# Self-attention of a decoder layer: denominators from the value product's weights, a new order on VectorE and ScalarE, and the residual addition on GpSimd

## The chip, the cores and the metric

The kernel runs on one core of one Trainium2 chip. The metric is the device time of one execution in microseconds. The kernel before takes 1735.19 us (median of 3 runs, 1734.19 to 1737.6). The engines are called PE (TensorE), DVE (VectorE), ACT (ScalarE), POOL (GpSimd) and SP (SyncE). Each has its own instruction stream, and semaphores join them.

## The reference, cut to what matters

Inputs are `x` (128 sequences of 64 tokens of 128 features, float32) and a context of the same shape. Three blocks follow each other, each with a layer norm ahead of it and its result added to `x`:

```python
x = x + attn(layernorm(x), Wq, Wk, Wv)         # self-attention: the stage that is changed
x = x + xattn(layernorm(x), ctx, ...)          # two LSTM cells with attention, 64 steps in sequence
x = x + ffn(layernorm(x), router_W, ...)       # top-1 of 8 experts

def attn(x, Wq, Wk, Wv):                       # 16 query heads of 8 features, one shared key and value head
    q = (x @ Wq.T).reshape(B, S, 16, 8).transpose(0, 2, 1, 3)
    k = x @ Wk.T;  v = x @ Wv.T
    p = softmax(einsum('bhqd,bkd->bhqk', q, k) / sqrt(8))
    return einsum('bhqk,bkd->bhqd', p, v).transpose(0, 2, 1, 3).reshape(B, S, 128)
```

## The kernel before, in words

The program has stages with a barrier between them: weights and context projections (to about 82 us), self-attention (to about 527 us), the second layer norm, the recurrence, and the experts. Only the self-attention stage is touched, lines 364 to 693.

All of `x` lies in SBUF as `X`. One pair of sequences fills 128 partitions (64 tokens each), so the stage works on 64 pairs. After a preparation (norm statistics, weights split into two float16 parts), each engine runs `step(i, u)` for i from -3 to 64; `run_steps` writes the first five and the last five steps out and puts the rest in a loop that holds two steps. In step i the engines work on several pairs at once:

- PE (L467): transposes the normalised rows of pair i+2 into `psK` (L473); scores of pair i+1, 32 small float16 products into `psSc` (L460); transposes `pv`, the value product of pair i-1, back into `psSc` (L487, four blocks); transposes the probabilities of pair i into `psT` (L492, eight blocks); projections of pair i+2 into `psQ` and `psK` and values of pair i+1 (all L453, by `split3`); and the value product of pair i (L520).
- The value product multiplies the transposed probabilities `prT` by two small stationary matrices of 32 columns: `VB` (for each of the two sequences and two heads, the 8 value features, zero on the other head's keys) and `ob` (ones in the same pattern, whose product is the softmax denominators). Both run over all 128 columns of `prT`, so of each result the half that combines a sequence's values with the other sequence's queries is thrown away. That makes 16 matmuls per pair for each matrix in instruction count (float32 products are issued as two), and `pv` has 512 columns: 256 of values and 256 of denominators.
- ACT (L537): `pv` copy of pair i-1 (L542), `xh`, the high part of the transposed input of pair i+2 (L546), two copies of `prT` (L551), `hq` (L557) and `hk` (L559), the high parts of the projections, and the exponential of pair i+1 (L563).
- DVE (L618): `xh` low part (L622), `xn` of pair i+3 (L628), `bn_stats` of the finished row of pair i-2 (L633), row maximum of the scores of pair i+1 (L642), reciprocal of the denominators (L648) and product into `yv` (L655) of pair i-1, each in two instructions of 64 partitions because the useful half of the columns differs by sequence, subtraction of the maximum (L664), `KS` (L670), `QS` (L672), `VB` (L678), and the addition of `yv` to `X` (L687).

Every engine takes its instructions in the order written. The waits that matter: `psK` of pair i+2 (L473) waits for `QS` and `VB` of DVE, since these read the same PSUM bank; ACT's `xh` waits for it, and DVE's `xh` for ACT's. The maximum (L642) waits for the scores and for the transposes of `pv` of pair i-1. `KS` waits for `hk`. The exponential waits for the subtraction, and the eight transposes (L492) of the next step wait for the exponential. GpSimd does nothing in this stage.

Of the kernel before, what the change touches and what calls it, by code (L numbers as in the profile page):

```python
# [14 lines left out]
P = 128  # L15
# [35 lines left out]
def decoder_kernel(nc, x, ctxT, wqT, wkT, wvT, wi0T, wh0T, bi0, bh0, wi1T, wh1T, bi1, bh1,  # L51
# [4 lines left out]
    with ExitStack() as persist:  # L56
# [307 lines left out]
        with ExitStack() as c2:  # L364
# [14 lines left out]
            ob = sb("ob", [P, 2, 2, DK])  # L379
# [10 lines left out]
            VB = sb("VB", [P, 2, 2, 2, DK])  # L390
# [3 lines left out]
            pv = sb("pv", [P, 512])  # L394
            rden = sb("rden", [P, NH])
            yv = sb("yv", [P, NH, DK])
# [32 lines left out]
            v_x1 = sem("v_x1")  # L429
# [6 lines left out]
            def run_steps(eng, step):  # L436
                for i in range(-3, 2):
                    step(i, i % 2)
                with eng.Fori(2, NPAIR - 5, 2) as i:
                    step(i, 0)  # L440
                    step(i + 1, 1)
                for i in range(NPAIR - 4, NPAIR + 1):
                    step(i, i % 2)

            with nc.Block() as block:
                @block.tensor
                def _(pe):
                    pe.wait_ge(v_c, 5)
# [18 lines left out]
                    def step(i, u):  # L467
# [11 lines left out]
                        if has(i - 1):  # L479
                            n = i - 1  # L480
                            pe.wait_ge(a_o, n + 1)
                            wait(pe, v_y, 2 * n)
                            if has(i) and not has(i + 1):
                                pe.wait_ge(v_sub, i + 1)
                            for k in range(4):
                                c0 = 256 + k % 2 * P
                                mm = nc.tensor.transpose(psSc[:, k // 2, c0:c0 + P], pv[:, k * P:(k + 1) * P], ident[:, :])  # L487
                            mm.then_inc(p_ot, 1)
# [38 lines left out]
                def _(act):  # L527
# [3 lines left out]
                    act.wait_ge(v_c, 5)  # L531
# [35 lines left out]
                def _(dve):  # L567
# [11 lines left out]
                    for b in range(2):  # L579
                        nc.vector.tensor_copy(ob[:, b, :, :], pm[:, :].unsqueeze(2).broadcast_to([P, 2, DK])).then_inc(v_c, 1)  # L580
                    dve.wait_ge(v_c, 5)
# [12 lines left out]
                    dve.wait_ge(v_c, 7)  # L594
# [23 lines left out]
                    def step(i, u):  # L618
                        if has(i + 2):
                            n = i + 2  # L620
                            dve.wait_ge(a_xh, n + 1)
                            nc.vector.scalar_tensor_tensor(xh[:, u, 1, :], psK[:, 0:P], S, xh[:, u, 0, :],  # L622
                                                           ALU.mult, ALU.subtract).then_inc(v_xl, 1)
                        if has(i + 3):
                            n = i + 3
                            wait(dve, p_xt, n - 1)
                            wait(dve, v_x1, i - 1)
                            nc.vector.tensor_scalar(xn[:, 1 - u, :], X[:, bass.ds(n * D, D)], mvf[:, bass.ds(n * 2, 1)],  # L628
                                                    rs[:, bass.ds(n, 1)], ALU.subtract, ALU.mult).then_inc(v_xn, 1)
                        if has(i - 2):  # L630
                            if not has(i + 3):
                                dve.wait_ge(v_x1, i - 1)
                            nc.vector.bn_stats(x1_stf[:, bass.ds((i - 2) * 6, 6)],  # L633
                                               X[:, bass.ds((i - 2) * D, D)]).then_inc(v_x1st, 1)
# [8 lines left out]
                        if has(i - 1):  # L643
                            n = i - 1
                            dve.wait_ge(p_ot, n + 1)
                            for b in range(2):
                                q = slice(64 * b, 64 * b + 64)
                                nc.vector.reciprocal(  # L648
                                    rden[q, :].rearrange("p (k h) -> p k h", h=2),
                                    psSc[q, 1, 256:512].rearrange("p (k b h d) -> p k b h d", b=2, h=2, d=DK)[:, :, b, :, 0]  # L650
                                ).then_inc(v_rd, 1)
                            dve.wait_ge(v_rd, 2 * n + 2)
                            for b in range(2):
                                q = slice(64 * b, 64 * b + 64)
                                nc.vector.tensor_tensor(  # L655
                                    yv[q, :, :].rearrange("p (k h) d -> p k h d", h=2),
                                    psSc[q, 0, 256:512].rearrange("p (k b h d) -> p k b h d", b=2, h=2, d=DK)[:, :, b, :, :],
                                    rden[q, :].rearrange("p (k h) -> p k h", h=2).unsqueeze(3).broadcast_to([64, 8, 2, DK]),
                                    ALU.mult).then_inc(v_y, 1)
# [7 lines left out]
                        if has(i + 2):  # L667
                            n = i + 2
                            dve.wait_ge(a_hq, 2 * n + 2)
                            nc.vector.scalar_tensor_tensor(KS[:, u, :], psK[:, P:2 * P], DOWN, hk[:, :],  # L670
                                                           ALU.mult, ALU.subtract)
                            nc.vector.scalar_tensor_tensor(QS[:, u, :], psQ[:, :], DOWN, hq[:, :],  # L672
                                                           ALU.mult, ALU.subtract).then_inc(v_qs, 1)
                        if has(i + 1):
# [4 lines left out]
                                VB[:, 1 - u, :, :, :],  # L679
# [10 lines left out]
                    dve.wait_ge(v_x1, NPAIR)  # L690
# [1033 lines left out]
```

## Time and profile before

| | |
|---|---|
| median of 3 runs | 1735.19 us |
| the profiled execution | 1734.93 us, span 1733.2 us |
| busy in the span: PE, DVE, ACT, POOL | 1453.0, 1191.0, 749.5, 401.6 us |
| mean granted TensorE clock, whole span | 0.929 |
| self-attention, 128 to 512 us: PE, DVE, ACT, POOL busy | 288.27, 319.47, 232.25, 0.00 of 384 us |
| mean granted TensorE clock there | 0.90 |

A granted clock of 1.00 is 2.4 GHz and 0.50 is 1.2 GHz. In the list of groups a line names the engine, the operation, the tile written and the tiles read, the shapes, the count, then busy time and mean duration of one, and the idle time of the engine before these instructions. In the timeline a line has start, duration, engine, line and tiles; consecutive instructions of one kind are merged (x2, x8), and brackets hold the idle time before and what ended it. Instructions of an engine overlap a little at their ends, so the distance between two starts is shorter than the first one's duration.

### The profile page before, as it was taken

The numbers are of one execution on the slowest core, as the hardware profiler recorded it, in microseconds if no ns is written. First come the engines' busy times: TensorE is split into PE (matmuls) and PEld (weight loads), VectorE is DVE, ScalarE is ACT, GpSimd is POOL, SyncE is SP. The second block draws the span as 40 slices with busy tenths as digits, with TensorE's granted clock in tenths as the row PEclk, the third lists the DMA queues.
The fourth block names the chain that finished last, engine by engine and source line by source line (L and its number), as shares of the span: only waits on it lengthen the run. The fifth ranks groups of instructions, "written<-read, shape, count | busy, mean of one in ns | idle before, by whom it ended". The sixth has DMA issues, their size and how long they took to land. (4 is left out here: it accounts for less than half of the span.)

```text
span 1733.2 us, 86487 instructions
## 1 busy us (share of the span) xinstructions
PE 1453.0 (84%) x34524; PEld 1264.6 (73%) x34525; DVE 1191.0 (69%) x4763; ACT 749.5 (43%) x2083; POOL 401.6 (23%) x1130
## 2 busy tenths in 40 slices
PE   1637777777775799999999999999999998669997
PEld 1426666666663699888888888888888888547665
DVE  5878888888887467666666666666667666545444
ACT  2435656565653244444444444444444443223332
POOL 0000000000000123333333333333333333313333
PEclk9768998988985799999999999999999999779999
DMA  6000000000003500000000000000000000032221
GB/s 231 1 1 1 0 0 0 0 0 0 0 1 99 179 11 19 15 14 14 14 14 14 14 14 14 14 14 14 14 14 14 14 14 16 18 95 74 73 75 42
DMA packets 42140, 50.64 MB, mean 29 GB/s; under 512 B 5674, under 2 KB 33836, under 8 KB 41800
## 3 DMA queue, kind: packets, MB, share of 16 engines
q1 hardware_dynamic: 35376, 34.98, 6.9%
q0 software_dynamic: 5376, 12.66, 2.1%
q10 hardware_dynamic: 1304, 1.86, 0.3%
q8 instruction: 55, 0.90, 0.2%
q14 instruction: 29, 0.24, 0.0%
HBM read 30.52 MB, written 19.48 MB: 29 GB/s over the span
## 5 line engine op out<-in xcount | busy, mean ns | idle before, releaser
L1059 PE MATMUL sc_ab<-h_a,KH 128*128 128x48 f16 (+2 forms) x4096 | 126.9, 184 | 5.3 <-issue 2.7
L1187 POOL MEMSET upper<- 128x128 f16 x1 | 0.2, 205 | 556.6 <-POOLq L66 556.6
L1059 PEld LDWEIGHTS sc_ab<-h_a,KH 128*128 128x128 f16 x4096 | 115.9, 97 | 9.9 <-issue 3.4
L1059 PE MATMUL sc_ab<-h_b,KH 128*128 128x48 f16 (+2 forms) x4096 | 122.1, 182 | 0.0
L986 PE MATMUL z_a<-h_a,WL 128*128 128x64 f16 x2304 | 113.2, 194 | 9.1 <-DVE h_a L1388 3.1
L473 PE MATMUL psK<-ident,xn 128*128 128x128 f32 x64 | 21.6, 338 | 117.1 <-DVE VB L678 90.5
L1109 PEld LDWEIGHTS mx_ab<-pmv_b,VH 128*128 128x128 f16 x4096 | 107.3, 96 | 16.4 <-DVE pmv_b L1439 16.3
L986 PE MATMUL z_b<-h_b,WL 128*128 128x64 f16 x2304 | 112.2, 193 | 7.0 <-issue 1.5
L1109 PE MATMUL mx_ab<-pmv_b,VH 128*128 128x16 f16 x4096 | 113.2, 170 | 5.5 <-DVE pmv_b L1439 0.8
L1109 PEld LDWEIGHTS mx_ab<-pmv_a,VH 128*128 128x128 f16 x4096 | 111.9, 97 | 1.0 <-DVE pmv_a L1439 1.0
L1132 ACT ACTIVATE gt_a<-z_a,sc 128x256 f32<-128x256 f32 x128 | 60.8, 475 | 119.7 <-PE z_a L986 119.7
L1109 PE MATMUL mx_ab<-pmv_a,VH 128*128 128x16 f16 x4096 | 112.1, 169 | 0.4 <-DVE pmv_a L1439 0.2
L1059 PEld LDWEIGHTS sc_ab<-h_b,KH 128*128 128x128 f16 x4096 | 112.4, 96 | 0.0
L1132 ACT ACTIVATE gt_b<-z_b,sc 128x256 f32<-128x256 f32 x128 | 60.8, 475 | 117.4 <-PE z_b L986 117.4
L551 ACT ACTIVATE prT<-psT 128x512 f32<-128x512 f32 x128 | 72.1, 596 | 89.0 <-PE psT L492 88.8
L1666 DVE TENSOR_TENSOR hb<-psH,b_sb 128x512 f32<-128x512 f32 x72 | 49.8, 692 | 87.1 <-PE psH L1599 76.8
L473 PEld LDWEIGHTS psK<-ident,xn 128*128 128x128 f32 x64 | 9.3, 145 | 132.9 <-issue 74.0
L986 PEld LDWEIGHTS z_a<-h_a,WL 128*128 128x128 f16 x2304 | 85.7, 98 | 26.2 <-DVE h_a L1396 11.9
L1576 POOL DMA_INDIRECT out<-ys,xr x72 | 70.8, 983 | 139.3 <-DVE ys L1678 138.4
L1613 PEld LDWEIGHTS psY<-X,hT 128*128 128x128 f32 x576 | 75.5, 191 | 33.6 <-issue 33.5
L986 PEld LDWEIGHTS z_b<-h_b,WL 128*128 128x128 f16 x2304 | 85.0, 97 | 20.1 <-DVE h_b L1396 12.7
L563 ACT ACTIVATE pr<-pr,s 128x1024 f32<-128x1024 f32 x64 | 73.4, 1148 | 48.0 <-DVE pr L664 47.8
(299 smaller groups left out, 3960.5 us busy)
## 6 DMA issues: line engine op xcount, KB each, us to landing
xr<-sorted_x SPq DMA_DIRECT2D x72, 129.0 KB, 2.1
XT<-in_ctxT SPq DMA_DIRECT2D x1, 4096.0 KB, 13.3
x_scratch<-X SPq DMA_DIRECT2D x1, 4096.0 KB, 15.9
x1r<-x_scratch SPq DMA_DIRECT2D x64, 64.0 KB, 1.8
X<-in_w SPq DMA_DIRECT2D x1, 2048.0 KB, 9.0
b_sb<-in_b SPq DMA_DIRECT2D x1, 2048.0 KB, 21.8
sorted_x<-zt SPq DMA_DIRECT2D x12, 129.0 KB
out<-ys,xr POOLq DMA_INDIRECT x72, 2.4
```

Of the source, the lines that this page charges most:

```text
L473: nc.tensor.transpose(psK[:, 0:P], xn[:, u, :], ident[:, :]).then_inc(p_xt, 1)
L551: nc.scalar.activation(prT[:, 4 * k:4 * k + 4, :].rearrange("p n t -> p (n t)"), psT[:, k, :], ACT.Copy).then_inc(a_pt, 1)
L563: nc.scalar.activation(pn, pn, ACT.Exp, scale=s2[:, 3:4]).then_inc(a_ex, 1)
L986: mm = nc.tensor.matmul(q.z[layer][:, j * GB:(j + 1) * GB], WL[:, blk + j, w, :], mov[m], start=False, stop=False, skip_group_check=True)
L1059: mm = nc.tensor.matmul(A.S[:, WIDE * n:WIDE * n + streamed(n)], KH[:, k, pair * P:(pair + 1) * P], A.h[1][:, 2 * n:2 * n + streamed(n) // ...
L1109: mm = nc.tensor.matmul(A.M[:, WIDE * n:WIDE * (n + 1)], VH[:, k, pair, :], A.pm[:, 2 * n:2 * n + WIDE // 2, :].rearrange("p b k -> p (b k)"),
L1132: nc.scalar.activation(L.gt[l][:, :, :].rearrange("p g b -> p (g b)"), L.z[l][:, 0:4 * GB], ACT.Tanh, scale=sc[:, I0 + l:I0 + l + 1]).then ...
L1187: pool.memset(upper[:, :], 1.0).then_inc(g_c, 1)
L1576: pool.indirect_dma_start(out_rows, bass.IndirectOffsetOnAxis(xr[:, u, AT_ROW:].bitcast(U32), 0), ys[:, u % 4, :], None, bounds_check=last ...
L1613: mm = nc.tensor.matmul(psY[:, u, 0:P], hT[:, u, c, :], w2_sb[:, bass.ds(col + c * P, P)], start=(c == 0), stop=(c == FC - 1))
L1666: nc.vector.tensor_tensor(hb[:, u, :], psH[:, u, :], b1_sb[:, bass.ds(col, FF)], ALU.add).then_inc(v_hb, 1)
```

## The change

- The ones of `ob` move into `VB`, which now has two halves per sequence: s = 0 the values, s = 1 the ones. `VB` has 32 columns per sequence (b = 0, 1), the ones are written once ahead of the loop (four copies in place of two), and each step writes only the values.
- The value product takes, for each sequence, its own `VB` and only that sequence's 64 columns of `prT`. There are as many matmuls as before, each over 64 columns instead of 128. `pv` has 256 columns, and two transposes instead of four bring it back (L487).
- In the result a sequence's values and denominators lie at the same columns on all partitions, so reciprocal and `yv` are one instruction each over 128 partitions. `yv` gets two buffers.
- The addition to `X` is an instruction of GpSimd, with a wait for `yv`; DVE's `bn_stats` waits for it, and `yv` for the addition before.
- ACT's copy of `pv` moves from the head of the next step to just ahead of the exponential of its own step.
- DVE begins a step with `bn_stats` and `xn`, and then does `xh`. `QS` comes ahead of `KS`, and waits for `hq` alone.
- The loop of each engine is written with a hint for the branch at its end.

```diff
@@ the loop
-                with eng.Fori(2, NPAIR - 5, 2) as i:
+                with nc.Fori(2, NPAIR - 5, 2, engines=[eng.engine], hint_back_edge=True) as i:
@@ GpSimd
+                @block.gpsimd
+                def _(pool):
+                    def step(i, u):
+                        if has(i - 1):
+                            n = i - 1
+                            pool.wait_ge(v_y, n + 1)
+                            xrow = X[:, bass.ds(n * D, D)].rearrange("p (a g d) -> p a g d", a=QA, g=4)
+                            nc.gpsimd.tensor_tensor(xrow, xrow, yv[:, 1 - u, :, :].rearrange("p (g a) d -> p a g d", g=4),
+                                                    ALU.add).then_inc(g_x1, 1)
+                    run_steps(pool, step)
@@ PE
-                            wait(pe, v_y, 2 * n)
+                            wait(pe, v_y, n)
-                            for k in range(4):
-                                c0 = 256 + k % 2 * P
-                                mm = nc.tensor.transpose(psSc[:, k // 2, c0:c0 + P], pv[:, k * P:(k + 1) * P], ident[:, :])
+                            for k in range(2):
+                                c0 = 256 + k * P
+                                mm = nc.tensor.transpose(psSc[:, 0, c0:c0 + P], pv[:, k * P:(k + 1) * P], ident[:, :])
...
-                                for w, c0 in ((VB[:, u, :, :, :], 0), (ob[:, :, :, :], 256)):
+                                for b in range(2):
+                                    c0 = half * P + 64 * b
                                     for j in range(4):
-                                        mm = nc.tensor.matmul(psT[32 * j:32 * j + 32, 0, c0 + half * P:c0 + (half + 1) * P],
-                                                              w.rearrange("p a b d -> p (a b d)"), prT[:, 4 * half + j, :],
+                                        mm = nc.tensor.matmul(psT[32 * j:32 * j + 32, 0, c0:c0 + 64],
+                                                              VB[:, u, b, :, :, :].rearrange("p s h d -> p (s h d)"),
+                                                              prT[:, 4 * half + j, 64 * b:64 * b + 64],
                                                               start=True, stop=True)
@@ ACT
-                        if has(i - 1):
-                            n = i - 1
-                            act.wait_ge(p_o, n + 1)
-                            wait(act, p_ot, n)
-                            nc.scalar.activation(pv[:, :], psT[:, 0, :], ACT.Copy).then_inc(a_o, 1)
...
+                        if has(i):
+                            act.wait_ge(p_o, i + 1)
+                            wait(act, p_ot, i)
+                            nc.scalar.activation(pv[:, :], psT[:, 0, 0:2 * P], ACT.Copy).then_inc(a_o, 1)
                         if has(i + 1):
                             act.wait_ge(v_sub, i + 2)
@@ DVE
+                        if has(i - 2):
+                            dve.wait_ge(g_x1, i - 1)
+                            nc.vector.bn_stats(...)
+                        if has(i + 3):
+                            ... xn
                         if has(i + 2):
                             ... xh
-                        if has(i + 3):
-                            ... wait(dve, v_x1, i - 1), xn
-                        if has(i - 2):
-                            ... bn_stats
...
-                            for b in range(2):
-                                ... reciprocal on partitions 64 * b to 64 * b + 64
-                            dve.wait_ge(v_rd, 2 * n + 2)
-                            for b in range(2):
-                                ... tensor_tensor into yv on partitions 64 * b to 64 * b + 64
+                            po = psSc[:, 0, 256:512].rearrange("p (k s h d) -> p k s h d", s=2, h=2, d=DK)
+                            rd = rden[:, :].rearrange("p (k h) -> p k h", h=2)
+                            nc.vector.reciprocal(rd, po[:, :, 1, :, 0]).then_inc(v_rd, 1)
+                            dve.wait_ge(v_rd, n + 1)
+                            wait(dve, g_x1, n - 1)
+                            nc.vector.tensor_tensor(
+                                yv[:, 1 - u, :, :].rearrange("p (k h) d -> p k h d", h=2), po[:, :, 0, :, :],
+                                rd.unsqueeze(3).broadcast_to([P, 8, 2, DK]), ALU.mult).then_inc(v_y, 1)
...
+                            dve.wait_ge(a_hq, 2 * n + 1)
+                            ... QS
                             dve.wait_ge(a_hq, 2 * n + 2)
                             ... KS
-                            ... QS
...
-                        if has(i - 1):
-                            n = i - 1
-                            dve.wait_ge(v_y, 2 * n + 2)
-                            xrow = X[:, bass.ds(n * D, D)].rearrange("p (a g d) -> p a g d", a=QA, g=4)
-                            nc.vector.tensor_tensor(xrow, xrow, yv[:, :, :].rearrange("p (g a) d -> p a g d", g=4),
-                                                    ALU.add).then_inc(v_x1, 1)
```

## Rows read from the trace of the kernel before

**Rows 1.** Busy time by stretch, columns as headed, most of the self-attention stage.

```profile
core 0: us, PE busy (x) PEld busy (x) DVE busy (x) ACT busy (x) POOL busy (x), PEclk, DMA share, GB/s
128.00:512.00 384.00, 288.27 (x6262) 249.55 (x6252) 319.47 (x780) 232.25 (x421) 0.00 (x0) 0.90 0.00 0
```

**Rows 2.** Groups of instructions by line, 128.38 to 512.66 us.

```profile
L563 ACT ACTIVATE pr<-pr,s 128x1024 f32<-128x1024 f32 x61 | 70.0, 1148 | 46.6 <-DVE pr L664 46.5
...
L542 ACT ACTIVATE pv<-psT 128x512 f32<-128x512 f32 x60 | 34.9, 581 | 0.0
...
L622 DVE SCALAR_TENSOR_TENSOR xh<-psK,xh 128x128 f16<-128x128 f32 x60 | 17.5, 292 | 44.0 <-ACT xh L546 44.0
```

**Rows 3.** Timeline of VectorE over one pair (start, duration, instruction, idle before).

```profile
302.59 0.18 DVE L678 TENSOR_TENSOR VB<-psK,pmv 128x32 f32<-128x32 f32 x1
302.69 0.28 DVE L687 TENSOR_TENSOR X<-X,yv 128x128 f32 x1
303.75 0.29 DVE L622 SCALAR_TENSOR_TENSOR xh<-psK,xh 128x128 f16<-128x128 f32 x1 [0.78 <-ACT xh L546]
304.07 0.35 DVE L628 TENSOR_SCALAR xn<-X,mv,rs 128x128 f32 x1
304.33 0.28 DVE L633 BATCH_NORM_STATS2 x_st<-X  x1
304.54 1.21 DVE L642 TENSOR_REDUCE pmx<-psSc 128x16 f32<-128x1024 f32 x1
305.66 0.53 DVE L648 RECIPROCAL rden<-psSc 64x16 f32<-64x16 f32 x2
306.22 0.61 DVE L655 TENSOR_TENSOR yv<-psSc,rden 64x128 f32<-64x128 f32 x2
306.87 1.23 DVE L664 TENSOR_TENSOR pr<-psSc,pmx 128x1024 f32<-128x1024 f32 x1
...
308.20 0.68 DVE L672 SCALAR_TENSOR_TENSOR QS<-psQ,hq 128x512 f16<-128x512 f32 x1
308.80 0.18 DVE L678 TENSOR_TENSOR VB<-psK,pmv 128x32 f32<-128x32 f32 x1
```

**Rows 4.** Timeline of the same pair, TensorE and ScalarE.

```profile
302.92 0.30 PE L473 MATMUL psK<-ident,xn 128*128 128x128 f32 x1 [0.94 <-DVE VB L678]
...
303.15 0.33 PE L460 MATMUL psSc<-KS,QS 32*64 32x64 f16 x32
...
304.10 1.04 PE L492 MATMUL psT<-ident,pr 128*128 128x128 f32 x8
...
304.73 1.08 ACT L551 ACTIVATE prT<-psT 128x512 f32<-128x512 f32 x2 [1.02 <-PE psT L492]
...
304.97 0.83 PE L453 MATMUL psQ<-xh,wst 128*128 128x128 f16 x12
...
306.01 0.69 ACT L557 ACTIVATE hq<-psQ,lo 128x512 f16<-128x512 f32 x1 [0.19 <-PE psK L453]
...
306.19 0.43 PE L520 MATMUL psT<-prT,VB 128*32 128x128 f32 x8
...
306.43 0.40 PE L520 MATMUL psT<-prT,ob 128*32 128x128 f32 x8
...
309.04 0.33 PE L473 MATMUL psK<-ident,xn 128*128 128x128 f32 x1 [1.76 <-DVE VB L678]
```

**Rows 5.** Timeline two pairs later, where nothing delays the transposes of pv.

```profile
315.78 0.18 DVE L678 TENSOR_TENSOR VB<-psK,pmv 128x32 f32<-128x32 f32 x1
...
316.60 0.66 PE L487 MATMUL psSc<-ident,pv 128*128 128x128 f32 x4
...
316.75 0.29 DVE L622 SCALAR_TENSOR_TENSOR xh<-psK,xh 128x128 f16<-128x128 f32 x1 [0.59 <-ACT xh L546]
```

**Rows 6.** Busy time by stretch, a stretch of low clock.

```profile
309.90:313.30 3.40, 3.40 (x20) 3.34 (x21) 2.94 (x8) 1.18 (x3) 0.00 (x0) 0.50 0.00 0
```

**Rows 7.** Timeline, ScalarE, the pair that this stretch falls in.

```profile
314.00 0.69 ACT L557 ACTIVATE hq<-psQ,lo 128x512 f16<-128x512 f32 x1 [0.66 <-PE psK L453]
```

**Rows 8.** Groups of instructions by line, GpSimd, the whole span.

```profile
L1264 POOL COPY TOK<-XN 128x128 f32<-128x128 f32 x64 | 18.7, 292 | 5.9 <-DVE XN L1333 5.9
```

More of the change, by code:

```diff
@@ L378, in decoder_kernel @@
             pmv = sb("pmv", [P, 2])
-            ob = sb("ob", [P, 2, 2, DK])
             st6 = sb("st6", [P, NPAIR, 6])
@@ L389, in decoder_kernel @@
             KS = sb("KS", [P, 2, P], F16)
-            VB = sb("VB", [P, 2, 2, 2, DK])
+            VB = sb("VB", [P, 2, 2, 2, 2, DK])
             pmx = sb("pmx", [P, 2, NH])
@@ L393, in decoder_kernel @@
             prT = sb("prT", [P, 8, P])
-            pv = sb("pv", [P, 512])
+            pv = sb("pv", [P, 2 * P])
             rden = sb("rden", [P, NH])
-            yv = sb("yv", [P, NH, DK])
+            yv = sb("yv", [P, 2, NH, DK])
             psSc = ps("psSc", [P, 4, 512])
@@ L428, in decoder_kernel @@
             v_y = sem("v_y")
-            v_x1 = sem("v_x1")
+            g_x1 = sem("g_x1b")
             v_x1st = sem("v_x1st")
@@ L445, in decoder_kernel @@
             with nc.Block() as block:
+                @block.gpsimd
[8 more added lines that the diff above has]
+                    run_steps(pool, step)
                 @block.tensor
                 def _(pe):
-                    pe.wait_ge(v_c, 5)
+                    pe.wait_ge(v_c, 7)
                     pe.wait_ge(v_w2, QA + 2)
@@ L530, in _ @@
                     act.wait_ge(v_s2, 6)
-                    act.wait_ge(v_c, 5)
+                    act.wait_ge(v_c, 7)
                     for a in range(QA + 1):
@@ L577, in _ @@
                                             AX.XY, ALU.add).then_inc(v_c, 1)
-                    for b in range(2):
-                        nc.vector.tensor_copy(ob[:, b, :, :], pm[:, :].unsqueeze(2).broadcast_to([P, 2, DK])).then_inc(v_c, 1)
-                    dve.wait_ge(v_c, 5)
+                    for u in range(2):
+                        for b in range(2):
+                            nc.vector.tensor_copy(VB[:, u, b, 1, :, :],
+                                                  pm[:, :].unsqueeze(2).broadcast_to([P, 2, DK])).then_inc(v_c, 1)
+                    dve.wait_ge(v_c, 7)
                     nc.vector.tensor_scalar(s2[:, 5:8], pw[:, 5:8], 2.0 ** -13, None, ALU.mult).then_inc(v_s2, 1)
@@ L593, in _ @@
                     nc.vector.tensor_tensor(lo[:, 1:2], m4[:, 1:2], m4[:, 3:4], ALU.add).then_inc(v_c, 1)
-                    dve.wait_ge(v_c, 7)
+                    dve.wait_ge(v_c, 9)
                     nc.vector.tensor_scalar(lo[:, :], lo[:, :], DOWN, None, ALU.mult).then_inc(v_s2, 1)
@@ L618, in step @@
                     def step(i, u):
+                        if has(i - 2):
+                            dve.wait_ge(g_x1, i - 1)
+                            nc.vector.bn_stats(x1_stf[:, bass.ds((i - 2) * 6, 6)],
+                                               X[:, bass.ds((i - 2) * D, D)]).then_inc(v_x1st, 1)
+                        if has(i + 3):
+                            n = i + 3
+                            wait(dve, p_xt, n - 1)
+                            nc.vector.tensor_scalar(xn[:, 1 - u, :], X[:, bass.ds(n * D, D)], mvf[:, bass.ds(n * 2, 1)],
+                                                    rs[:, bass.ds(n, 1)], ALU.subtract, ALU.mult).then_inc(v_xn, 1)
                         if has(i + 2):
@@ L623, in step @@
                                                            ALU.mult, ALU.subtract).then_inc(v_xl, 1)
-                        if has(i + 3):
[L625 to L629, printed above, removed]
-                        if has(i - 2):
[L631 to L634, printed above, removed]
                         if has(i + 1):
@@ L645, in step @@
                             dve.wait_ge(p_ot, n + 1)
-                            for b in range(2):
[L647 to L651, printed above, removed]
-                            dve.wait_ge(v_rd, 2 * n + 2)
[L653 to L659, printed above, removed]
+                            po = psSc[:, 0, 256:512].rearrange("p (k s h d) -> p k s h d", s=2, h=2, d=DK)
[6 more added lines that the diff above has]
+                                rd.unsqueeze(3).broadcast_to([P, 8, 2, DK]), ALU.mult).then_inc(v_y, 1)
                         if has(i + 1):
@@ L668, in step @@
                             n = i + 2
+                            dve.wait_ge(a_hq, 2 * n + 1)
+                            nc.vector.scalar_tensor_tensor(QS[:, u, :], psQ[:, :], DOWN, hq[:, :],
+                                                           ALU.mult, ALU.subtract)
                             dve.wait_ge(a_hq, 2 * n + 2)
                             nc.vector.scalar_tensor_tensor(KS[:, u, :], psK[:, P:2 * P], DOWN, hk[:, :],
-                                                           ALU.mult, ALU.subtract)
-                            nc.vector.scalar_tensor_tensor(QS[:, u, :], psQ[:, :], DOWN, hq[:, :],
                                                            ALU.mult, ALU.subtract).then_inc(v_qs, 1)
@@ L678, in step @@
                             nc.vector.tensor_tensor(
-                                VB[:, 1 - u, :, :, :],
+                                VB[:, 1 - u, :, 0, :, :],
                                 psK[:, 256:272].rearrange("p (b d) -> p b d", b=2).unsqueeze(2).broadcast_to([P, 2, 2, DK]),
@@ L682, in step @@
                                 ALU.mult).then_inc(v_vb, 1)
-                        if has(i - 1):
-                            n = i - 1
-                            dve.wait_ge(v_y, 2 * n + 2)
-                            xrow = X[:, bass.ds(n * D, D)].rearrange("p (a g d) -> p a g d", a=QA, g=4)
-                            nc.vector.tensor_tensor(xrow, xrow, yv[:, :, :].rearrange("p (g a) d -> p a g d", g=4),
-                                                    ALU.add).then_inc(v_x1, 1)
                     run_steps(dve, step)
-                    dve.wait_ge(v_x1, NPAIR)
+                    dve.wait_ge(g_x1, NPAIR)
                     nc.vector.bn_stats(x1_st[:, NPAIR - 1, :], Xp[:, NPAIR - 1, :]).then_inc(v_x1st, 1)
```

## The prediction

> **What bounds the kernel now.** I first took busy time by stretch: between 128 and 512 us VectorE is busy 319 of 384 us, TensorE 288, ScalarE 232, GpSimd not at all, and the mean granted TensorE clock is 0.90 [rows 1]. No engine is full, so the order of the work decides. The groups by line give the rhythm: 60 times `xh` (L622) in 384.28 us, 6.40 us for a pair, and before it VectorE idles 44.0/60 = 0.73 us, waiting for ScalarE [rows 2]. The timeline shows the ring that closes: VectorE works without a gap from `xh` (303.75) to the addition to `X` (302.69 in the pair before), its `VB` lets TensorE transpose into `psK` (302.92), ScalarE copies, and VectorE's next `xh` starts [rows 3, 4]. From one `VB` (302.59) to the next (308.80) is 6.21 us. The reader is to see that ScalarE and TensorE wait inside this ring. What raises 6.21 to 6.40 is the clock: for 309.9 to 313.3 us it is 0.50, that is 1.2 GHz [rows 6], and in that pair `hq` comes 314.00 - 309.04 = 4.96 us after the `psK` transpose where at 2.4 GHz it came 306.01 - 302.92 = 3.09 us after it [rows 4, 7]. At 0.90 mean, low clock holds a fifth of the stretch: 77 us, or some 22 stretches of 3.4 us in 60 pairs.
>
> **The change part by part.** I lay out the new pair from `VB`'s start as time 0, at 2.4 GHz.
>
> *From `VB` to the maximum.* Now it takes 304.54 - 302.59 = 1.95 us. Of that, `xh` starts 316.75 - 315.78 = 0.97 after `VB` where nothing is in its way and 1.16 in rows 3, where the `pv` copy of 0.58 us stood ahead of ScalarE's `xh`; then come `xn` and `bn_stats` [rows 2, 3, 5]. In the new order the addition is gone, and `bn_stats` (start to start 0.21) and `xn` (at most 0.35) run in the wait, from about 0.10 to 0.66, so they cost nothing below 0.97. If that cover went they would cost 0.5. `xh` runs 0.97 to 1.26. The maximum also waits for the transposes of `pv`: these start at 316.60 - 315.78 = 0.82 without waiting (the copy was made a step earlier), four last 0.66 and a single one 0.30 [rows 4, 5], so their starts are (0.66 - 0.30) / 3 = 0.12 apart, and two end at 0.82 + 0.42 = 1.24. With 0.10 for the handover (VB's end 302.77 to `psK` 302.92 is 0.15, an upper end) the maximum starts at 1.34. This wait is what is late next, ahead of `xh` by under 0.1.
>
> *From the maximum to `VB`.* Now 308.80 - 304.54 = 4.26 us [rows 3]. Two reciprocals take 306.22 - 305.66 = 0.56 and become one of 0.28; two products take 0.65 and become one, 0.32 (elements per partition are the same). The subtraction, and `KS` and `QS` in whichever order, keep their durations. So 4.26 - 0.28 - 0.33 = 3.65. At both ends: if an instruction over 128 partitions took as long as the two over 64, nothing is gained, 4.26; below 3.65 there is nothing, as the order is the same.
>
> Sum: 1.34 + 3.65 = 4.99 us for a pair.
>
> *What must hold for this.* (a) TensorE: two transposes of `pv` fewer bring L492 to 0.82 + 0.24 = 1.06; the projections follow 0.87 later at 1.93, `hq` 1.04 after them at 2.97 (304.97 to 306.01), done at 3.66; `QS` wants it at 1.34 + 1.12 + 0.28 + 0.32 + 1.14 = 4.20 (1.14 is the subtraction's 1.23 less an overlap of about 0.1, as between the maximum's 1.21 and the 1.12 to the reciprocals): 0.5 to spare. (b) The value product starts 1.22 after the projections, at 3.15. Eight matmuls of 128 columns take 306.43 - 306.19 = 0.24, four groups 0.88 with 128 columns and 0.44 if time goes with columns. I take the half, as in the 32 scores of 64 columns the starts lie within 0.33 us. It ends at 3.8 with a last latency of 0.2. (c) ScalarE then has `hk` (to 3.92), `pv` with 256 columns, between `hk`'s 128 and the 0.58 of 512, about 0.43, to 4.3, and the exponential, which wants the subtraction's end at 4.31. It runs 1.15 from 4.35, to 5.50, which is 0.51 of the next pair; `xh` of ScalarE wants to start at 0.66 (0.33 for `psK`'s start, 0.30, a handover). 0.15 to spare. Here the moved copy sits ahead of the exponential in ScalarE's queue, and behind both stand `xh`, `prT` and `hq`; if the product keeps its 0.88, the exponential ends 0.3 late, passes the 0.15, and the ring (half of the rest comes back) grows to about 5.06.
>
> *GpSimd's addition.* The trace has no such instruction. It is not below VectorE's 0.28 [rows 3]; the nearest of GpSimd is a copy of 128x128 float32 at 0.292 [rows 8]; two inputs I bound by twice that plus a handover, 0.8. I take 0.5. `yv` ends at 3.05, `bn_stats` of the next step wants the sum at 4.99 + 0.10, so 2.0 us hide it at either end. Behind that wait VectorE's `xn` and `xh` are queued; above 2.0 each microsecond is paid. The wait of `yv` is a pair old. The four set-up copies in place of two, at under 0.2 each, and three handovers to GpSimd in the last steps, where nothing hides them, cost about 1 us; shorter last steps give about that back.
>
> *The branch hint and the order inside the loop.* `xn` now starts 0.32 after `xh`, of 0.29; I cost the hint at nothing, between -0.1 and +0.1 a pair: VectorE's branch now lies under 0.8 us of issued `KS` and `VB` work.
>
> *The clock.* A fall to 1.2 GHz costs more than before, since slack is gone: `hq` came 1.87 later [rows 4, 7], about 0.25 of it from two transposes that no longer exist; less the 0.5 to spare that is 1.1 us, and the exponential behind it up to 0.3 more, 1.4 a fall. Whether it falls: it fell after TensorE had idled 1.76 us and not after 0.94 [rows 4, 6]. In the new pair TensorE idles from 3.8 to 4.99 + 0.33, 1.5 us. That lies between. I take one fall in 20 pairs (0.07) and the mean of the product's two ends (0.04): 5.10 us a pair.
>
> **Sum.** (6.40 - 5.10) x 60 = 78 us out of 1734.93 (span 1733.2 plus 1.7 around it, 0.26 under the median of the runs). Against the median: 1735.2 - 78 = about 1657 us.
>
> **A rule beside the rows.** The value product's eight matmuls of 128 columns start 30 ns apart at most [rows 4], and the 32 scores of 64 columns lie in 0.33 us, 10 ns apart. The Trainium skill, "TensorE: Matmul & The Clock Gate", section "Wait — 56ns, not 53.3ns?", says that matmuls never start closer than about 25 ns however few columns they have. By it halving the columns gives nothing, by the row of the scores it gives half; the scores disagree with it, though they use other tiles of the array than the product.
>
> **The rivals.** *Issue-bound product.* The value product keeps 0.88: 5.06 us a pair, TensorE idles 1.1 us, near the 0.94 after which the clock stayed up. For it: other tiles than the scores. 80 us gained, 1655; it is inside the forecast's own range.
>
> *The clock falls as often as now.* 22 falls in 60 pairs at 1.4 us on 4.99: 5.50 a pair, 54 us gained, 1681. For it: 1.5 us of idling is nearer to 1.76 than to 0.94. Against it: after a fall TensorE is late and idles less.
>
> *Another wait.* The single reciprocal and product save nothing (5.6 a pair), or the exponential, behind `pv`, holds up ScalarE by 0.5 us or more: 5.6, 48 us gained, 1687; with falls on top up to 1715.
>
> *TensorE at 1.2 GHz in every pair.* Then `hq`'s path is the ring: 4.99 + 1.4 = 6.4 a pair if each pair has one fall of 3.4 us, no gain; and with all of TensorE's work at half clock `hq` starts at 5.0 + 0.6, `VB` at 6.6 + 0.2 and the exponential behind it, 6.8: 24 us slower, 1759. It decides from one fall a pair on. For it: the thinner work. Against it: busy share (about 3.5 of 4.99 us) is no lower than now.
>
> **How the numbers follow.** Forecast with the issue-bound product 0.60 (4.9 to 5.2 us a pair, 1647 to 1665, its own range); falls as now 0.20; another wait 0.12; 1.2 GHz throughout 0.05; the rest, a gain spent elsewhere to within 0.2%, 0.03. Range 1645 to 1700: the lower end is the forecast with the hint's best 0.1 a pair and both handovers shorter, the upper takes in falls as now and most of another wait. Change under 0.2%, 3.5 us, is about what a measurement of this kernel cannot tell from none. Faster 0.92, same 0.03, slower 0.05.
>
> **What would show it.** The distance between two `xh` at 5.0 to 5.2 us; one reciprocal of about 0.25 and one `yv` of about 0.29; the idle time before VectorE's `xh` at 0.3 or less, and some before the maximum; the product's groups of eight 0.11 us apart (0.22: issue-bound); GpSimd's addition under 1 us and no wait of `bn_stats` for it; granted clock at or over 0.95 in the stage. I am wrong if the clock is below 0.9, if the exponential waits for `pv` and not for the subtraction, or if `QS` waits for `hq` in most pairs.

## The result, and the profile after

The changed kernel takes 1653.68 us (median of 4 runs, 1652.7 to 1656.33) against 1736.36 us (4 runs, 1734.19 to 1737.6): a ratio of 0.9529, 95% interval 0.9513 to 0.9544, so 83 us less where 78 were forecast. The profiled executions have spans of 1651.8 and 1733.2 us, 81.4 apart. From the first `xh` of VectorE to the last it is now 322.2 us (108.72 to 430.91) and was 400.5 (107.94 to 508.42): 78.3 of the 81.4 us lie there. Behind the last `xh` the stage ends after 15.5 us instead of 18.4.

Busy time by stretch of the kernel after, with the columns of [rows 1]:

```profile
128.00:430.00 302.00, 226.59 (x6063) 198.82 (x6052) 267.21 (x595) 218.30 (x417) 27.08 (x59) 0.94 0.00 0
164.60:167.80 3.20, 3.20 (x27) 3.04 (x26) 2.81 (x4) 1.19 (x2) 0.45 (x1) 0.54 0.00 0
```

VectorE is busy 88% of the stage, where it was 83% [rows 1], and the clock is at 0.94. The timeline of VectorE in the kernel after, over one pair, answers to [rows 3]:

```profile
287.06 0.18 DVE L684 TENSOR_TENSOR VB<-psK,pmv 128x32 f32<-128x32 f32 x1
287.15 0.28 DVE L634 BATCH_NORM_STATS2 x_st<-X  x1
...
287.36 0.33 DVE L639 TENSOR_SCALAR xn<-X,mv,rs 128x128 f32 x1
...
288.03 0.29 DVE L644 SCALAR_TENSOR_TENSOR xh<-psK,xh 128x128 f16<-128x128 f32 x1 [0.35 <-ACT xh L553]
...
288.35 1.22 DVE L653 TENSOR_REDUCE pmx<-psSc 128x16 f32<-128x1024 f32 x1
...
289.49 0.25 DVE L659 RECIPROCAL rden<-psSc 128x16 f32<-128x16 f32 x1
...
289.77 0.29 DVE L662 TENSOR_TENSOR yv<-psSc,rden 128x128 f32<-128x128 f32 x1
...
289.98 1.22 DVE L669 TENSOR_TENSOR pr<-psSc,pmx 128x1024 f32<-128x1024 f32 x1
...
291.11 0.68 DVE L675 SCALAR_TENSOR_TENSOR QS<-psQ,hq 128x512 f16<-128x512 f32 x1
...
291.71 0.28 DVE L678 SCALAR_TENSOR_TENSOR KS<-psK,hk 128x128 f16<-128x128 f32 x1
291.90 0.18 DVE L684 TENSOR_TENSOR VB<-psK,pmv 128x32 f32<-128x32 f32 x1
```

From `VB` to `VB` it is 4.84 us. `bn_stats` and `xn` now stand where the wait was, which has shrunk from 0.78 to 0.35. From the maximum to `VB` it is 291.90 - 288.35 = 3.55, before 4.26. The other engines in the same pair, answering to [rows 4, 8]:

```profile
287.38 0.30 PE L483 MATMUL psK<-ident,xn 128*128 128x128 f32 x1 [1.40 <-DVE VB L684]
...
287.87 0.44 PE L497 MATMUL psSc<-ident,pv 128*128 128x128 f32 x2
...
290.06 0.69 ACT L564 ACTIVATE hq<-psQ,lo 128x512 f16<-128x512 f32 x1 [0.19 <-PE psK L463]
...
290.24 0.65 PE L531 MATMUL psT<-prT,VB 128*32 128x64 f32 x32
290.25 0.46 POOL L452 TENSOR_TENSOR X<-X,yv 128x128 f32 x1 [4.39 <-DVE yv L662]
...
290.96 0.38 ACT L570 ACTIVATE pv<-psT 128x256 f32<-128x256 f32 x1
...
291.24 1.14 ACT L574 ACTIVATE pr<-pr,s 128x1024 f32<-128x1024 f32 x1
```

The 32 matmuls of the value product lie in 0.65 us. With the last one's latency of 0.2 taken off, their starts are about 0.45 / 31 = 14 ns apart. GpSimd needs 0.46 us and is done 1.3 us before anyone asks. The next group shows a pair of the same kernel in which the clock falls (the second line of the first group is this stretch, at a mean of 0.54). TensorE had idled 1.40 us before it, as it does in every second pair, with and without a fall:

```profile
163.53 0.30 PE L483 MATMUL psK<-ident,xn 128*128 128x128 f32 x1 [1.40 <-DVE VB L684]
...
164.17 0.29 DVE L644 SCALAR_TENSOR_TENSOR xh<-psK,xh 128x128 f16<-128x128 f32 x1 [0.34 <-ACT xh L553]
...
168.57 0.69 DVE L675 SCALAR_TENSOR_TENSOR QS<-psQ,hq 128x512 f16<-128x512 f32 x1 [1.03 <-ACT hq L564]
...
170.38 0.29 DVE L644 SCALAR_TENSOR_TENSOR xh<-psK,xh 128x128 f16<-128x128 f32 x1
```

This pair takes 6.21 us. `QS` waits 1.03 us for `hq`, which comes late behind transposes and projections at half clock. Of the 63 distances between `xh`, 11 inside the loop are of this kind (6.09 to 6.21); the others alternate between 4.79 and 4.91, and the one behind a fall is 4.72 to 4.84. No distance is near 5.1: only their mean is.

### The profile page after: what moved, and what is told of

Read it like the earlier page. It is cut to its first block and busy times, and to the rows that moved or that the text cites. A ratio compares the mean times of both kernels' runs of the same rounds, so it can differ in the third digit from the quotient of the medians.

```text
span 1651.8 us, 86284 instructions
## 1 busy us (share of the span) xinstructions
PE 1395.1 (84%) x34396; PEld 1215.9 (74%) x34397; DVE 1139.0 (69%) x4573; ACT 737.2 (45%) x2083; POOL 430.7 (26%) x1194
## 5 line engine op out<-in xcount | busy, mean ns | idle before, releaser
L452 POOL TENSOR_TENSOR X<-X,yv 128x128 f32 (+1 forms) x64 | 29.4, 459 | 412.4 <-DVE yv L662 412.4
L1109 PEld LDWEIGHTS mx_ab<-pmv_b,VH 128*128 128x128 f16 x4096 | 107.0, 96 | 16.3 <-DVE pmv_b L1439 16.3
L1258 POOL DMA_INDIRECT sorted_x<-TOK,slot x64 | 70.3, 1098 | 46.1 <-DVE a_a L1456 22.3
```

The source lines that it names most:

```text
L1109: mm = nc.tensor.matmul(A.M[:, WIDE * n:WIDE * (n + 1)], VH[:, k, pair, :], A.pm[:, 2 * n:2 * n + WIDE // 2, :].rearrange("p b k -> p (b k)"),
L1258: pool.indirect_dma_start(xs_dram, bass.IndirectOffsetOnAxis(slot[:, u:u + 1], 0), TOK[:, u, :], None).then_inc(d_sc[u], 16)
```

## The experiments

All twelve were timed in three sets (e1 to e4, e5 to e8, e9 to e12), each on one chip together with the kernel before, which took 1772.6, 1772.1 and 1737.2 us there. The difference between the sets lies outside the changed stage: what is left of a profiled span beside the stretch from first to last `xh` is 1364 to 1374 us in the first two sets and 1329 to 1333 in the third. So I compare ratios, and that stretch, called the stage here. Ratios of different sets compare only to some 0.004, as e4 and e10 show below. "At 2.4 GHz" are the pairs that no low clock touches; "falls" are the whole stretches of 3.4 us at 1.2 GHz between 130 us and the last `xh` in the profiled execution.

| kernel | ratio (95% interval) | stage, us | pair at 2.4 GHz | falls |
|---|---|---|---|---|
| before | 1 | 400.5 | 6.20 and 6.31 | 22 |
| after | 0.9529 (0.9513 to 0.9544) | 322.2 | 4.79 and 4.91 | 11 |
| e1 product undone | 0.9912 (0.9885 to 0.9939) | 381.5 | 5.39 to 5.87 | 20 |
| e2 orders undone | 0.9766 (0.9745 to 0.9788) | 363.7 | 5.20 and 5.39 | 27 |
| e3 addition on VectorE | 0.9547 (0.9524 to 0.9570) | 322.6 | 4.81 and 5.05 | 8 |
| e4 after, 3 filling matmuls | 0.9466 (0.9445 to 0.9486) | 308.8 | 4.79 and 4.91 | 0 |
| e5 product alone | 0.9768 (0.9742 to 0.9795) | 363.4 | 5.20 and 5.40 | 27 |
| e6 orders alone | 0.9893 (0.9868 to 0.9917) | 383.3 | 5.55 to 5.74 | 22 |
| e7 pv copy back | 0.9527 (0.9506 to 0.9548) | 323.8 | 4.82 and 5.00 | 10 |
| e8 KS first, 3 filling | 0.9343 (0.9324 to 0.9361) | 283.0 | 4.42 | 0 |
| e9 before, 3 filling | 0.9916 (0.9891 to 0.9940) | 390.0 | 6.14 and 6.30 | 0 |
| e10 after, 1 filling | 0.9424 (0.9402 to 0.9446) | 308.7 | 4.79 and 4.91 | 0 |
| e11 no hint | 0.9514 (0.9494 to 0.9533) | 320.3 | 4.79 and 4.91 | 10 |
| e12 xh first | 0.9686 (0.9660 to 0.9712) | 352.1 | 5.16 and 5.39 | 22 |

**The product undone.**

```diff
-  for b in range(2): ... VB[:, u, b, :, :, :] x prT[:, 4 * half + j, 64 * b:64 * b + 64]
+  for w in (VB, ob): ... w x prT[:, 4 * half + j, :]
   (and pv of 512, four transposes, reciprocal and yv in halves, as before the change)
```

> The changed kernel with the value product as before: VB and ob over all 128 columns, pv of 512 columns, four transposes, reciprocal and yv in two instructions of 64 partitions each. The new orders, the addition on GpSimd and the hint stay. Theory (VectorE's ring sets the pair; each instruction taken from it counts in full): 0.28 for the reciprocal and 0.33 for yv come back, and the two transposes more delay the maximum by 0.2: 4.85 becomes 5.45 to 5.65 us at 2.4 GHz, with some falls of the clock about 5.8 a pair, 60 x 0.7 = 42 us more than the changed kernel: about 1696 us. Rival (most of the gain comes from the orders and the idle time that they close): at most 20 us more, under 1675.

It gives back 59 us of the stage, well above the 42 expected and far above the rival's. Between falls its pairs take 5.54 us on average, inside the 5.45 to 5.65 of the expectation and no more than 4.85 and the 0.7 that VectorE's run is longer. The rest is the clock: it falls 20 times instead of 11, and a pair with a fall takes up to 7.07 us. Why it costs more is in the timeline of e1, in a pair behind a fall:

```profile
292.50 0.60 ACT L569 ACTIVATE pv<-psT 128x512 f32<-128x512 f32 x1 [0.84 <-PE psT L531]
...
292.99 1.14 ACT L573 ACTIVATE pr<-pr,s 128x1024 f32<-128x1024 f32 x1
...
294.03 0.27 ACT L552 ACTIVATE xh<-psK 128x128 f16<-128x128 f32 x1
...
294.33 0.29 DVE L641 SCALAR_TENSOR_TENSOR xh<-psK,xh 128x128 f16<-128x128 f32 x1 [1.42 <-ACT xh L552]
```

The long product ends late, ScalarE's copy waits 0.84 us for it, and the exponential and `xh` queue behind the copy, though the subtraction has long been done. VectorE's `xh` waits 1.42 us. This is the product's hidden part in the gain: with the new place of the copy, a short product is what keeps the exponential on time when the clock falls.

**The orders undone, the product alone, the orders alone.**

```diff
 e2:  the order of xh, xn, bn_stats; KS, QS; and the pv copy as before; the rest as after
 e5:  e2, and X + yv on VectorE, no hint
 e6:  e1, and X + yv on VectorE, no hint
```

> The changed kernel with VectorE's and ScalarE's orders as before: xh ahead of xn and bn_stats, KS ahead of QS, the copy of pv at the head of the next step. Product, addition on GpSimd and hint stay. Theory (bn_stats and xn, 0.21 + 0.26 start to start, leave the wait for xh and are paid in full, and the pv copy of 0.38 stands ahead of ScalarE's xh): 4.85 becomes 5.35 to 5.5, 60 x 0.55 = 33 us more than the changed kernel, about 1687 us. Rival (the work taken away is the gain, and the order is nearly free): under 10 us more.

> The kernel before with the new value product alone (VB with ones, 64 columns, two transposes, one reciprocal, one yv); old orders, addition on VectorE, no hint. Theory (it takes 0.7 us from VectorE's run between maximum and VB, but xh still waits 0.75 us with xn and bn_stats behind it): pairs of 5.2 to 5.5 us at 2.4 GHz and, with TensorE idle for 1.7 us in each, a fall in every third pair as without the order in the last runs: mean 5.75 to 5.9, 30 to 40 us less than before, ratio 0.977 to 0.983. Rival (the product carries what its undoing cost, 59 us of the stage): ratio 0.966.

> The kernel before with the new orders alone (bn_stats and xn ahead of xh, QS ahead of KS, the copy of pv ahead of the exponential); old product, addition on VectorE, no hint. Theory (the idle time before xh closes at 2.4 GHz, but the value product of 0.88 us ends late, the copy of pv of 0.58 waits for it and the exponential behind it, so each fall is paid in two pairs): mean 6.0 to 6.15 a pair, 15 to 22 us less than before, ratio 0.987 to 0.991. Rival (the order gives what its undoing cost, 42 us): ratio 0.976.

Undoing the orders costs 41 us (33 expected, 10 by the rival). Here too the pairs at 2.4 GHz do not make the surplus: they grow by less than expected, to 5.20 and 5.39, and the clock falls 27 times. Alone the product brings 37 us of the stage and the orders 17, in or at the edge of what was expected; together with the addition and the hint they bring 78. So 24 us exist only where both are there.

These 24 us are the clock's. The pairs that no low clock touches take 6.25 us on average before, 5.31 with the product alone, 5.64 with the orders alone and 4.85 with both. Over 60 pairs that would be 56, 37 and 84 us, so without falls both together would give no more than the sum of each. What the means over all pairs (6.40, 5.77, 6.10, 5.10) lie above these is about 9 us before, 28 in e5, 28 in e6 and 15 after: with either change alone the falls cost some 19 us more, with both 6. This is worked out from the profiled executions; e5 and e6 were not run with the idle time filled.

With the product alone VectorE still idles before `xh` and then waits for `hk`, and the clock is at 0.86. The waits of VectorE in e5, 130 to 400 us (total, times, longest):

```profile
DVE xh L625 <- ACT xh L547: 27.1, 47, 0.7
DVE KS L665 <- ACT hk L560: 22.0, 23, 1.1
```

With the orders alone it is ScalarE's copy that waits for the product; the same view of e6:

```profile
ACT pv L558 <- PE psT L520: 18.2, 44, 0.9
DVE xh L630 <- ACT xh L541: 8.1, 15, 0.9
```

**The addition back on VectorE.**

```diff
-  @block.gpsimd ... nc.gpsimd.tensor_tensor(xrow, xrow, yv ...)
+  nc.vector.tensor_tensor(xrow, xrow, yv ...)      # behind VB, at the end of the step
```

> The changed kernel with the addition to X back on VectorE at the end of the step, no GpSimd; all else stays. Theory (VectorE idles 0.25 to 0.35 us ahead of xh, and the addition behind VB fills just this idle time, 0.2 to 0.3 start to start): 4.85 grows by 0 to 0.1, 0 to 6 us more than the changed kernel, 1654 to 1660 us, VectorE's idle time before xh near 0. Rival (an instruction more on the bound engine costs its length): 0.28 x 60 = 17 us more, about 1671.

The stage is 0.4 us longer, and the ratio's interval meets that of the changed kernel. The addition fills the idle time ahead of `xh`:

```profile
291.67 0.28 DVE L682 TENSOR_TENSOR X<-X,yv 128x128 f32 x1
292.21 0.29 DVE L623 BATCH_NORM_STATS2 x_st<-X  x1 [0.26 <-DVE X L682]
...
292.83 0.28 DVE L633 SCALAR_TENSOR_TENSOR xh<-psK,xh 128x128 f16<-128x128 f32 x1
```

It does not fit in quite: in every second pair `bn_stats` waits 0.26 us for the addition, and the pairs at 2.4 GHz are 0.08 us longer on average, some 5 us of the stage. This profile has 8 falls where that of the changed kernel has 11, which gives most of it back. So GpSimd's part of the change is worth nothing in the time measured, and by this estimate some 5 us where the clock does not fall; no run has both.

**The copy of pv back at the head of the step.**

```diff
-  if has(i):      ... pv copy, ahead of the exponential
+  if has(i - 1):  ... pv copy, first in step i
```

> The changed kernel with only ScalarE's copy of pv back at the head of the next step; VectorE's new order, product, GpSimd and hint stay. Theory (the exponential begins with the subtraction's end in both, and the 0.33 us that it frees ahead of the exponential comes back between it and ScalarE's xh, where only about 0.2 us are free): 0.1 to 0.2 us a pair more, 6 to 12 us over the changed kernel, ratio 0.956 to 0.960. Rival (the copy's place is what the order gave): ratio 0.97 or more.

A miss of the expectation: 1.6 us of the stage, ratio as the changed kernel's. The pairs at 2.4 GHz are 0.06 us longer on average, as VectorE's maximum now waits in 29 of them for the transposes of `pv`; that is 3 to 4 us of the stage, and one fall fewer gives part of it back.

**xh ahead of xn and bn_stats again.**

```diff
-  bn_stats(i - 2); xn(i + 3); xh(i + 2)
+  xh(i + 2); xn(i + 3); bn_stats(i - 2)
```

> The changed kernel with xh ahead of xn and bn_stats again, as the kernel before has it; QS ahead of KS, the pv copy's new place, product and GpSimd stay. Theory (this is the part of the orders that counts: 0.21 + 0.26 us leave the wait, which becomes 0.75, and TensorE idles 1.7 and more, so that falls come in every third pair as with both orders undone): pairs of 5.2 to 5.4 at 2.4 GHz, mean 5.6 to 5.8, ratio 0.973 to 0.978. Rival (QS ahead of KS carries a good part, as it does without hk): under 0.968.

It costs 30 us of the stage; the ratio, 0.9686, is below the expected 0.973 to 0.978, and its interval reaches into the rival's range, under 0.968. The pair at 2.4 GHz grew as forecast (5.16 and 5.39). Since both orders undone cost 41.5 and the copy's place 1.6, `QS` ahead of `KS` and what joins the parts are left with 10 us, which no run shows by itself. The pairs at 2.4 GHz differ by 0.02 us only, so these 10 us too lie nearly all in the pairs with low clock, of which e2 has 27 and e12 has 22. From 130 to 420 us, `KS` stands in front in e2 and waits for `hk`, where in e12 `QS` waits for `hq` (first e2, then e12):

```profile
DVE KS L676 <- ACT hk L571: 20.1, 21, 1.1
```

```profile
DVE QS L675 <- ACT hq L564: 11.8, 18, 0.9
```

**Without the hint.**

```diff
-  with nc.Fori(2, NPAIR - 5, 2, engines=[eng.engine], hint_back_edge=True) as i:
+  with eng.Fori(2, NPAIR - 5, 2) as i:
```

> The changed kernel with the loops' branches without the hint. Theory (the body of each engine's loop fits and VectorE's branch lies under issued work): same time as the changed kernel within 0.1 us a pair, ratio 0.951 to 0.957. Rival (the hint saves a fetch in each turn): 0.2 us or more a turn of two pairs, ratio 0.957 or more.

The time is the same. The alternation of 4.79 and 4.91 stays too, so it isn't a fetch that the hint would hide.

**Filling TensorE's idle time.** Matmuls whose result nobody uses follow the value product, three in e4, e8 and e9, one in e10. In e4 and e10 nothing else changes. e8 comes below. e9, against what its expectation says, also has two buffers for `yv`, and in it `bn_stats` waits for the addition and not `xn`.

```diff
                             mm.then_inc(p_o, 1)
+                            for _ in range(3):
+                                nc.tensor.matmul(psT[:, 1, :], wst[:, 0, 0, :], KH[:, 0, 0:512], start=True, stop=True)
```

> The changed kernel with three float16 matmuls of 512 columns behind the value product, into a half of psT that nobody reads before the next step overwrites it; 0.64 us of TensorE's idle 1.4 us is filled in each step. It computes nothing that is used. Theory (the falls of the clock to 1.2 GHz cost 1.3 us each and come from the idle time): no or nearly no falls between 128 and 430 us, granted clock 0.99 or more, 4.85 us a pair, 11 x 1.3 = 14 us less than the changed kernel, about 1639 us. Rival (the long pairs come from something else, or more work on TensorE delays psK): no change or slower, clock as before at 0.94.

> The kernel before with the three filling matmuls behind the value product, their result unused; nothing else changed. Theory (the falls cost the kernel before only 0.4 to 0.6 us each, as VectorE's run hid the rest): all pairs at 6.20 and 6.30, 60 x (6.39 - 6.25) = 8 us less than before, ratio 0.995, granted clock 0.99 or more between 130 and 400 us. With it the comparison without falls reads 6.25 before and 4.85 after, 84 us, against 78 with them. Rival (filling delays psK in this kernel, as the product ends later): ratio 1.00 or more.

> The changed kernel with one filling matmul of 512 columns, 0.21 us, in place of three. Theory (the idle time of 1.3 to 1.4 us lies close to where the clock stays up): with 1.1 us of idle time no or nearly no falls, 4.85 a pair, ratio 0.946 to 0.948 like the three. Rival (only a large filling helps): falls in every sixth pair as without, ratio 0.953.

Busy time by stretch, first e4, then e10:

```profile
130.00:420.00 290.00, 255.44 (x6262) 196.77 (x6260) 265.83 (x594) 219.19 (x419) 27.65 (x60) 1.00 0.00 0
```

```profile
130.00:400.00 270.00, 214.90 (x5735) 177.62 (x5733) 248.47 (x556) 204.48 (x390) 25.72 (x56) 1.00 0.00 0
```

The falls are gone in e4, e9 and e10, and one matmul does it. Here is TensorE in e10:

```profile
287.97 0.39 PE L537 MATMUL psT<-KH,wst 128*128 128x512 f16 x1
289.43 0.30 PE L483 MATMUL psK<-ident,xn 128*128 128x128 f32 x1 [1.08 <-DVE VB L686]
```

It idles 1.08 us, and the clock stays at 2.4 GHz, where 1.40 let it fall in some pairs. The longest idle time alone doesn't decide: e3 has 1.55 in every second pair and falls 8 times. Eleven falls cost the changed kernel 322.2 - 308.8 = 13.4 us, 1.2 each. In e9 the stage is 10.5 us shorter, but some 2 of them are not the clock's: the shorter of its two pairs at 2.4 GHz went from 6.20 to 6.14, perhaps by the wait that moved. That leaves 22 falls at about 0.4 each. e9's ratio lies under the 0.995 expected, and e10's 0.9424 under its 0.946 to 0.948.

By the ratios e4 saves 0.0063, 11 us, and e10 0.0105, 18 us, though their stages are equal. The two ran in different sets. Against a kernel of its own set, with falls and all but the same stage as the changed one, e4 saves 1693.3 - 1677.8 = 15.5 us (e3) and e10 1651.5 - 1636.8 = 14.7 us (e11), so the 7 us between the ratios are no effect of the filling.

**A faster version.** VectorE does `KS` and `VB` ahead of `QS`, the `psK` transposes wait for these two alone, TensorE transposes `pv` ahead of the scores, and three matmuls fill.

```diff
 DVE: KS ... .then_inc(v_ks, 1); VB ... .then_inc(v_vb, 1); QS ... .then_inc(v_qs, 1)
 PE:  psK transpose waits for v_ks in place of v_qs; the two transposes of pv, then the scores
 PE:  the projections wait for v_qs (they overwrite psQ)
```

> A version meant to be faster: the changed kernel with the three filling matmuls, and on VectorE KS and VB ahead of QS (KS has its own semaphore), so that the psK transposes wait for KS and VB alone and run, with ScalarE's xh, under QS; TensorE does the transposes of pv ahead of the scores. Theory (the rest of the ring's idle time closes until the exponential and ScalarE's xh behind it bound it): 4.5 to 4.65 us a pair, no falls, 28 to 35 us less than the changed kernel, ratio 0.933 to 0.937. Rival (ScalarE's chain of hq, hk, pv, exponential and xh bounds it already): 4.8 or more, ratio 0.945 or more.

The ratio is as expected, and every pair of the loop takes 4.42 us, under the 4.5 to 4.65 given. Against e4, which has the same filling, the stage is 25.8 us shorter; what each of the two new orders gives was not run. VectorE of e8 behind `VB`:

```profile
282.92 0.18 DVE L685 TENSOR_TENSOR VB<-psK,pmv 128x32 f32<-128x32 f32 x1
283.02 0.68 DVE L691 SCALAR_TENSOR_TENSOR QS<-psQ,hq 128x512 f16<-128x512 f32 x1
...
283.62 0.28 DVE L638 BATCH_NORM_STATS2 x_st<-X  x1
...
283.82 0.33 DVE L643 TENSOR_SCALAR xn<-X,mv,rs 128x128 f32 x1
...
284.18 0.29 DVE L648 SCALAR_TENSOR_TENSOR xh<-psK,xh 128x128 f16<-128x128 f32 x1
...
284.39 1.22 DVE L657 TENSOR_REDUCE pmx<-psSc 128x16 f32<-128x1024 f32 x1
```

No wait is left: the ring is VectorE's own work. Here the addition on GpSimd should count in full, since no idle time is there to take it; that is argued and wasn't run.

## Why the prediction was right

The forecast pair was 5.10 us; the mean from the fifth `xh` to the last is 5.10 (before 6.40). The mechanism was right: a shorter run of VectorE and a covered wait. That the number fits to 0.01 us is luck. The ring was forecast 0.14 us too long, the falls of the clock at 0.15 a pair too little, the product's 0.04 was nothing, and the errors all but cancelled.

*VectorE's run from the maximum to `VB`* was forecast at 3.65 and is 3.55. The reciprocal saves the 0.28 of the sum. The product `yv` saves 0.44 and not 0.33: the subtraction starts 0.21 behind the single instruction, where it started 0.65 behind the first of the two [rows 3].

*From `VB` to the maximum* I had 1.34, and it is 1.29. The moved instructions cost nothing, as said, and the orders count because they stand in the wait (e12). The wait I named as next, the maximum's for TensorE, hardly shows; what is left is the one before `xh`. The ring at 2.4 GHz is 4.85 where the sum said 4.99.

VectorE's waits in the kernel after, 128 to 430 us (total, times, longest):

```profile
DVE xh L644 <- ACT xh L553: 14.6, 48, 0.3
DVE QS L675 <- ACT hq L564: 11.7, 11, 1.2
...
DVE pmx L653 <- PE psSc L497: 0.8, 3, 0.4
```

*The clock* was the mis-sized term. I took one fall in 20 pairs, 0.07 us a pair; there were 11 in some 60, and they cost 13.4 us, 0.22 a pair. The granted clock is 0.94, a little under the 0.95 that was to show the forecast. The price of a fall was right (up to 1.4 forecast; 6.15 against 4.85 in the pair, 1.2 with the slightly shorter pair behind it), and so was the place, `QS` waiting for `hq`, eleven times. That the idle time (1.24 and 1.40 in turn, where 1.5 was forecast) lay between the two cases was true, but not that this made falls rare. The two cases were thin ground. The 0.94 of [rows 4] stands in a pair just behind a fall (296.2 to 299.6 us), in which TensorE is late. And elsewhere in the kernel before, 1.89 us of idle time brought no fall:

```profile
187.80 0.30 PE L473 MATMUL psK<-ident,xn 128*128 128x128 f32 x1 [1.89 <-DVE VB L678]
```

```profile
187.00:193.50 6.50, 4.23 (x104) 3.62 (x104) 5.57 (x14) 4.12 (x8) 0.00 (x0) 1.00 0.00 0
```

e10 shows how near the edge the changed kernel is.

*The value product* goes with its columns: 0.45 us for 32 matmuls of 64 columns, where 32 of 128 took 0.88. So the issue-bound rival is out, and the term of 0.04 for it was nothing. The Trainium skill ("TensorE: Matmul & The Clock Gate", section "Wait — 56ns, not 53.3ns?") gives about 25 ns as the least distance between starts; this trace, whose product lies in four column groups of the array, has 14 ns on average and disagrees with it there. The length of the product I had priced by what it delays, ScalarE's copy and the exponential behind it, at 0.07 us a pair at 2.4 GHz. e1 shows that this is dear only in and behind a fall, a case that the sum did not have.

*GpSimd* (0.5 forecast, 0.46 measured, over 1 us to spare) holds nothing up, as costed, and *the hint* is nothing (e11). The last steps, which I set at nothing net, gave 2.9 us. With the product alone they take 15.8 us behind the last `xh`, with the orders alone 16.3, so either part gives most of it; how, no run separates.

*The rivals.* Falls as often as before: half of it came true, 11 and not 22, and e4 against the changed kernel measures it. By its own terms the worst case of the rival of another wait is 5.6 + 0.51 = 6.11 us a pair, 1718 us and not 1715, and 4.9 to 5.2 us a pair are 1645 to 1663; neither bears on the result. Another wait did not appear in the kernel, but it is what e1 and e6 show when the product is long. TensorE at 1.2 GHz in every pair did not come.

## What to carry to other kernels

Where one engine runs a ring with another engine's reply in it, first look for own work that can stand in the wait, and then shorten the run; here either alone gave half or less, and nearly a third of the gain needed both, because with one alone the falls of the clock took part of it back. An instruction moved to a free engine is worth little or nothing while the bound engine has idle time at that very place. After tightening such a ring, check TensorE's idle time per turn: a few useless matmuls in it can be cheaper than a fall of the clock, whose price grows as slack goes (0.4 us before, 1.2 after). When two versions differ in the number of falls, compare the turns without a fall too; the time alone hid 0.08 us a pair in e3.

## What the runs showed of the hardware

One filling matmul of 512 columns in a pair of 4.85 us keeps the granted clock at 1.00 (e10, 130 to 400 us) instead of 0.94 (the changed kernel, 128 to 430 us), with 1.1 us of idle time left ahead of the `psK` transpose. Two VectorE instructions on 64 partitions each, with the one behind them, cost more than twice one on 128: for `yv` 0.65 to the start of the next [rows 3], against 0.21 after. 32 float32 matmuls of 64 columns in four column groups start 14 ns apart on average.
